# A graph-attention layer on one core: one wait per operation, rings of eight, destinations over 102 partitions

## Chip, core and metric

The kernel runs on 1 core of one Trainium2 chip. The metric is device time in microseconds (us), the median of 3 runs; lower is better.

## What is computed

The reference is one graph-attention layer with a residual and a layer norm. N = 12500 nodes have 96 features; E = 412500 edges are sorted by destination; there are 8 heads of 12 features.

```python
Q, K, V = x @ Wq + bq, x @ Wk + bk, x @ Wv + bv         # (N, 8, 12) each
Ee      = edge_attr @ We + be                            # (E, 8, 12)
score = exp(clip(sum(K[src] * Q[dst] / sqrt(12) * Ee, over 12), -5, 5))
wV = segment_sum(V[src] * score, dst, N)
Z  = segment_sum(score, dst, N)
out = layernorm(x + wV / (Z + 1e-6))
```

## The kernel before

**Tiling.** The edges go in C = 806 chunks of 512 edges, four groups of 128 (G = 4). As the edges are sorted, the destinations of one chunk nearly always lie in one window of 32 nodes (WIN), so a chunk's queries are picked, and its messages summed, by matmuls with one-hot matrices. Weights and sums are float32; the query table is kept as three bfloat16 parts, hence 96 rows (SEL = 32 x 3) of a one-hot for the queries.

**Stages.** A first stage (about 160 us) makes the K/V and Q tables in HBM, the tables of windows and indices, and a copy of the destinations as 16-bit numbers. The main stage runs 806 steps, one per chunk. The last stage divides by Z and normalizes.

**One step of the main stage**, each engine in its own order, tied by semaphores alone (no planner; the order is written out by hand in one `step` function per engine):

- POOL (L546) issues four indirect DMAs (L553) that gather the 512 rows of K and V (768 bytes each) into one of 8 slots (RING). For the gather of chunk s it waits until the messages of chunk s - 8 are made (`msg_ready` >= s - 7), so it runs at most seven chunks ahead of the messages. This wait is the same before and after.
- SP (L412) loads the query windows four at a time, when `pe_step` allows.
- ACT (L784) for step s: waits for `pe_step` >= s + 1 and for `score_ready`, makes the exponential of chunk s - 1 (L791), waits that one-hot t has been made, makes the transposed one-hot of chunk s + 4 in two activations (L798, L801), issues the load of four chunks of destinations (L376, every fourth step), copies indices (L757, every fourth), and issues the load of four chunks of edge attributes (L361, three DMAs, every fourth step, after a wait on `ea_turned`).
- PE (L655) for step s: the edge projection (L665, 4 matmuls that appear as 8, float32 in two passes), the query selection (L670, 4), and the summing of chunk s - 5 (L678, shown as 8). The last one raises `pe_step`. There is no wait inside the summing.
- DVE (L930) for step s: waits for `pe_step` >= s + 1 and for the gather of chunk s, then kqe = k x q (L944), the one-hot of chunk s - 1 (L947), kqe x e (L952), messages of chunk s - 1 (L956, after the exponential; raises `msg_ready`), the reduction over 12 (L963), the addition into the accumulator (L971), the clip (L975), and the transposition of the attributes of chunk s + 4 (L980, raises `ea_turned`).

Rings before: one-hots for queries 4 (`ohT`), messages 4 (`msg`), one-hots for sums 4, attributes 16, destinations 8, indices 16.

At the start SP issues two groups of attributes and two of destinations (L419 to L423) before it stores the query table (L428).

## Time and profile before

| | |
|---|---|
| median of 3 runs | 5284.68 us (5274.52 to 5292.71) |
| the profiled execution | 5282.84 us |
| its span, first to last instruction | 5281.0 us |
| mean granted TensorE clock | 0.507 of full speed |
| busy: PE / DVE / ACT / POOL | 59% / 47% / 25% / 60% |
| mean HBM traffic | 115 GB/s |

No engine is busy for more than 60% of the span, and the shares are flat over it. The page's part 4, the chain of waits that ended last, tells which engine the time follows; the view of waits tells what each engine waited for; the timelines show one round of the pipeline. "issue" is time in which an engine waited for nothing that the profile shows; "remote" is a release of which the profile does not show the sender.

### The profile page before, as it was taken

The page shows a single profiled execution, that of the slowest core. Times are in us where ns is not written, and L with a number is a line of the kernel's source. Part 1 is how long each engine was busy: PE and PEld are TensorE (multiplying, and loading weights), DVE is VectorE, ACT ScalarE, POOL GpSimd, SP SyncE. Part 2 cuts the span into 40 slices and gives each one's busy share as a digit, 9 for nine tenths or more (in the row PEclk, how much of TensorE's full clock was granted, in tenths as well). Part 3 has the DMA queues.
Part 4 walks back from the last instruction along what each step waited for, and adds up shares of the span by engine and source line. Part 5 has one row for each costly group of instructions (what it writes and reads, how often), then busy time and mean ns, then how long its engine had stood idle before and what let it go on. Part 6 is the DMA issues. An engine that isn't in the chain of part 4 may idle for free.

```text
span 5281.0 us, 65022 instructions
## 1 busy us (share of the span) xinstructions
PE 3108.9 (59%) x16776; PEld 3038.4 (58%) x16777; DVE 2471.5 (47%) x6851; ACT 1338.4 (25%) x2885; POOL 3184.4 (60%) x3332
## 2 busy tenths in 40 slices
PE   6656556556565556655565555655555556665655
PEld 5655555555565555555565555555555555565555
DVE  3544444444444444444444444444444444444446
ACT  3322222222222222222222222222222222222224
POOL 4465666666656666666666666666566656666664
PEclk7555555555555555555555555555555555555555
DMA  7654545554544554444555544455444545454443
GB/s 211 136 113 109 114 111 114 113 115 109 117 112 110 114 114 114 110 111 110 116 113 114 114 110 111 112 114 114 109 114 111 115 111 115 110 117 110 112 108 97
DMA packets 1532837, 607.55 MB, mean 115 GB/s; under 512 B 1394171, under 2 KB 1455174, under 8 KB 1532579
## 3 DMA queue, kind: packets, MB, share of 16 engines
q10 hardware_dynamic: 1245734, 233.93, 23.6%
q0 software_dynamic: 155616, 321.69, 23.0%
q1 hardware_dynamic: 131459, 51.62, 4.0%
q8 instruction: 9, 0.15, 0.0%
q14 instruction: 19, 0.16, 0.0%
HBM read 584.51 MB, written 22.46 MB: 115 GB/s over the span
## 4 chain that ended last, share of the span: by engine, by line
PE 55%; issue 40%; DVE 1%; another core or an unknown queue 1%; DMA 1%; SPq 1%; ACT 0%; DVEq 0%; POOL 0%; ACTq 0%; POOLq 0%
PE bank L665 28%; PE bank L678 21%; PE bank L670 5%; DMA kv_mem<-in_x_dram 1%; PE bank L613 0%; DVE y_stats L1060 0%; SPq L361 0%; DMA q_table<-ea_mem 0%; SPq L395 0%; DVE kqe L952 0%; DVE raw_score L963 0%; SPq L428 0%; SPq L381 0%; DVE z_inv L1049 0%
## 5 line engine op out<-in xcount | busy, mean ns | idle before, releaser
L553 POOL DMA_INDIRECT kv_mem<-kv_table,src_idx x3224 | 3117.8, 967 | 2037.2 <-DVE msg L956 1043.3
L678 PE MATMUL bank<-oh,msg 128*104 128x32 f32 x6448 | 1302.8, 337 | 1611.2 <-issue 1610.5
L678 PEld LDWEIGHTS bank<-oh,msg 128*104 128x104 f32 x6448 | 1282.1, 285 | 1586.5 <-issue 1585.4
L665 PE MATMUL bank<-w_e,eaT 97*128 97x96 f32 x6448 | 1663.8, 429 | 328.1 <-issue 321.8
L665 PEld LDWEIGHTS bank<-w_e,eaT 97*128 97x128 f32 x6448 | 1494.7, 330 | 400.6 <-issue 399.0
L944 DVE TENSOR_TENSOR kqe<-kv_mem,bank 128x384 f32<-128x384 f32 x806 | 427.8, 531 | 2677.1 <-remote 2133.4
L791 ACT ACTIVATE msg<-score 128x32 f32<-128x32 f32 x806 | 184.9, 229 | 3798.9 <-remote 2633.6
L798 ACT ACTIVATE away<-dst_b,minus_id 96x512 bf16<-96x512 int16 x806 | 572.4, 710 | 6.1 <-PE bank L670 3.6
L980 DVE STREAM_TRANSPOSE eaT<-ea_mem 96x512 f32<-96x512 f32 x806 | 564.3, 700 | 0.0
L670 PE MATMUL bank<-q_win,ohT 96*128 96x96 bf16 x3224 | 449.0, 280 | 144.2 <-issue 138.4
L801 ACT ACTIVATE ohT<-away 96x512 bf16<-96x512 bf16 x806 | 507.5, 630 | 25.4
L670 PEld LDWEIGHTS bank<-q_win,ohT 96*128 96x128 bf16 x3224 | 410.4, 157 | 154.7 <-issue 146.3
L956 DVE TENSOR_TENSOR msg<-kv_mem,msg 128x384 f32<-128x384 f32 x806 | 441.7, 548 | 16.9 <-issue 12.9
L963 DVE TENSOR_REDUCE raw_score<-kqe 128x32 f32<-128x384 f32 x806 | 438.1, 544 | 0.0
L952 DVE TENSOR_TENSOR kqe<-kqe,bank 128x384 f32<-128x384 f32 x806 | 437.6, 543 | 0.0
L947 DVE TENSOR_TENSOR oh<-iota,rel 128x128 f32<-128x128 f32 x806 | 223.9, 278 | 0.0
L975 DVE TENSOR_SCALAR score<-raw_score 128x32 f32<-128x32 f32 x806 | 183.0, 227 | 0.2
L971 DVE TENSOR_TENSOR accT<-bank,accT 104x32 f32 x806 | 144.3, 179 | 4.1 <-PE bank L678 2.9
L639 PE MATMUL bank<-w_kvq,accT 97*125 97x96 f32 x200 | 37.5, 373 | 30.2 <-issue 17.8
L639 PEld LDWEIGHTS bank<-w_kvq,accT 97*125 97x125 f32 x200 | 36.1, 285 | 31.7 <-issue 19.4
L576 POOL TENSOR_TENSOR kv_mem<-kv_mem,spare 125x384 f32<-125x384 f32 x25 | 25.0, 999 | 44.5 <-DVE kv_mem L1054 44.5
L724 PE MATMUL bank<-ident,accT 104*125 104x104 f32 x100 | 30.6, 464 | 25.2 <-DVE kv_mem L1054 23.0
(90 smaller groups left out, 473.1 us busy)
## 6 DMA issues: line engine op xcount, KB each, us to landing
ea_mem<-in_edge_attr_dram ACTq DMA_DIRECT2D x591, 256.0 KB
dst_b<-dst_by_chunk ACTq DMA_DIRECT2D x199, 384.0 KB
kv_mem<-kv_table,src_idx POOLq DMA_INDIRECT x3224
q_win<-q_table SPq DMA_DIRECT2D x806, 19.9 KB
kv_table<-kv_mem SPq DMA_DIRECT2D x25, 336.0 KB
q_table<-ea_mem SPq DMA_DIRECT2D x25, 252.0 KB
kv_mem<-in_x_dram SPq DMA_DIRECT2D x25, 168.0 KB
spare<-in_x_dram SPq DMA_DIRECT2D x25, 168.0 KB
```

The costliest lines, as they stand in the source:

```text
L553: pool.indirect_dma_start(kv[:, slot, g, :], None, kv_dram[:, :], bass.IndirectOffsetOnAxis(ap=src_idx[:, u, g:g + 1], axis=0)).then_inc(k ...
L665: nc.tensor.matmul(e_ps[v][:, g * D:(g + 1) * D], eaT[:, v, g * P:(g + 1) * P], w_e[:, :], start=True, stop=True)
L670: last = nc.tensor.matmul(q_ps[v][:, g * D:(g + 1) * D], ohT[:, v, g * P:(g + 1) * P], q_win[0:SEL, u, :], start=(g == 0), stop=(g == G - ...
L678: last = nc.tensor.matmul(sum_ps[v], msg[:, w, g, :], oh[:, w, g, :], start=(g == 0), stop=(g == G - 1), skip_group_check=True)
L798: nc.scalar.activation(away[:, :], dst_b[:, w, :], ACT.Abs, bias=minus_id[:, bass.ds(t, 1)]).then_inc(away_done, 1)
L801: nc.scalar.activation(ohT[:, v, :], away[:, :], ACT.Relu, bias=1.0, scale=-1.0).then_inc(ohT_built, 1)
L944: nc.vector.tensor_tensor(kqe[:, :, :], kv[:, ua, :, 0:D], q_ps[v][:, 0:G * D].rearrange("p (g d) -> p g d", g=G), ALU.mult).then_inc(kq_d ...
L947: nc.vector.tensor_tensor(oh[:, um % DEPTH, :, :], iota[:, 0:WIN].unsqueeze(1).to_broadcast((P, G, WIN)), rel[:, bass.ds(m * G, G)].unsque ...
L952: nc.vector.tensor_tensor(kqe[:, :, :], kqe[:, :, :], e_ps[v].rearrange("p (g d) -> p g d", g=G), ALU.mult).then_inc(kqe_done, 1)
L956: nc.vector.tensor_tensor(msg[:, um % DEPTH, :, 0:D].rearrange("p g (h d) -> p g h d", d=HD), kv[:, um, :, D:2 * D].rearrange("p g (h d) - ...
L963: nc.vector.tensor_reduce(raw_score[:, :], kqe[:, :, :].rearrange("p g (h d) -> p (g h) d", d=HD), AX_X, ALU.add).then_inc(heads_summed, 1)
L980: nc.vector.transpose(eaT[0:D, v, :], ea[:, w, :]).then_inc(ea_turned, 1)
```

## The change

What it does, part by part:

1. PE: the wait for the query one-hot (`ohT_built`) moves from the query matmuls to the second group of the edge projection; in the steps after the last chunk the wait on `acc_added` goes.
2. ACT: the waits on `pe_step` and on `ohT_built` go; `away` has two buffers; `ohT` has eight (MSG_RING); the attribute loads are issued one residue earlier (u % 4 == 0, 16 chunks ahead, not 15), and their wait on `ea_turned` goes except at step 0.
3. DVE: new order of the same eight operations: one-hot, accumulator addition, k x q, x e, messages, reduction, transposition, clip. The waits on its own `heads_summed`, `acc_added` and on `exp_done` before the clip go; one wait on `score_ready` stands before the addition. The one-hot raises no semaphore.
4. `msg` has eight buffers, not four.
5. The destinations are loaded into 102 partitions, not 96.
6. Start: SP waits for the stored destinations first, loads attribute group 0 alone, and group 1 only after the query table is stored, with groups 2 and 3. Several small buffers share memory.

```diff
@@ load_destinations
-                "(a c r) -> a c r", a=1, c=count).to_broadcast((SEL, count, CHUNK))).then_inc(dst_b_in[h], 16)
+                "(a c r) -> a c r", a=1, c=count).to_broadcast((SEL_LOAD, count, CHUNK))).then_inc(dst_b_in[h], 16)
@@ sync
             sp.wait_ge(src_turned, NJ)
+            sp.wait_ge(dst16_stored, 32)
             load_edges(sp, 0, 0)
-            sp.wait_ge(dst16_stored, 32)
-            load_edges(sp, EA_GROUP, 1)
...
-            for g in range(2, EA_RING // EA_GROUP):
+            for g in range(1, EA_RING // EA_GROUP):
                 load_edges(sp, g * EA_GROUP, g)
@@ tensor: step
                     for g in range(G):
+                        if g == 1:
+                            pe.wait_ge(ohT_built, s + 1)
                         nc.tensor.matmul(e_ps[v][:, g * D:(g + 1) * D], eaT[:, v, g * P:(g + 1) * P],
                                          w_e[:, :], start=True, stop=True)
-                    pe.wait_ge(ohT_built, s + 1)
                     landed(pe, q_win_in, s, u, 16)
...
-                    pe.wait_ge(acc_added, n - DEPTH + 1)
                     pe.wait_ge(msg_ready, n + 1)
@@ scalar: step
-                m, t, v = s - 1, s + DEPTH, u % DEPTH
-                if not isinstance(s, int) or s >= 0:
-                    act.wait_ge(pe_step, s + 1)
+                m, t, w = s - 1, s + DEPTH, (u + DEPTH) % RING
                 if not isinstance(s, int) or 0 <= m < C:
                     act.wait_ge(score_ready, m + 1)
...
-                    at_least(act, ohT_built, t)
-                    nc.scalar.activation(away[:, :], dst_b[:, w, :], ACT.Abs,
+                    nc.scalar.activation(away[:, u % 2, :], dst_b[0:SEL, w, :], ACT.Abs,
                                          bias=minus_id[:, bass.ds(t, 1)]).then_inc(away_done, 1)
                     act.wait_ge(away_done, t + 1)
-                    nc.scalar.activation(ohT[:, v, :], away[:, :], ACT.Relu, bias=1.0, scale=-1.0).then_inc(ohT_built, 1)
+                    nc.scalar.activation(ohT[:, w, :], away[:, u % 2, :], ACT.Relu, bias=1.0, scale=-1.0).then_inc(ohT_built, 1)
...
-                if u % EA_GROUP == 1 and (not isinstance(s, int) or 0 <= s and s + EA_AHEAD < C):
-                    act.wait_ge(ea_turned, s + EA_AHEAD - EA_RING + EA_GROUP)
+                if u % EA_GROUP == EA_AHEAD % EA_GROUP and (not isinstance(s, int) or 0 <= s and s + EA_AHEAD < C):
+                    if isinstance(s, int) and s == 0:
+                        act.wait_ge(ea_turned, EA_GROUP)
                     load_edges(act, s + EA_AHEAD, (u + EA_AHEAD) % EA_RING // EA_GROUP)
@@ vector: step
                     dve.wait_ge(pe_step, a + 1)
-                if scores:
-                    landed(dve, kv_in, a, ua, 16 * G)
-                    at_least(dve, heads_summed, a)
-                    nc.vector.tensor_tensor(kqe[:, :, :], kv[:, ua, :, 0:D],
-                                            q_ps[v][:, 0:G * D].rearrange("p (g d) -> p g d", g=G), ALU.mult).then_inc(kq_done, 1)
                 if messages:
                     nc.vector.tensor_tensor(oh[:, um % DEPTH, :, :], iota[:, 0:WIN].unsqueeze(1).to_broadcast((P, G, WIN)),
                                             rel[:, bass.ds(m * G, G)].unsqueeze(2).to_broadcast((P, G, WIN)),
-                                            ALU.is_equal).then_inc(oh_built, 1)
+                                            ALU.is_equal)
+                if not isinstance(s, int) or 1 <= a <= C:
+
+                    dve.wait_ge(score_ready, a)
+                elif a > C:
+                    dve.wait_ge(acc_added, n)
+                if sums:
+                    if base is None:
+                        base = dve.value_load(base_tab[0:1, bass.ds(n, 1)], min_val=0, max_val=N - 1)
+                    acc = accT[0:DZ, bass.ds(base, WIN)]
+                    nc.vector.tensor_tensor(acc, sum_ps[v], acc, ALU.add).then_inc(acc_added, 1)
                 if scores:
+                    landed(dve, kv_in, a, ua, 16 * G)
+                    nc.vector.tensor_tensor(kqe[:, :, :], kv[:, ua, :, 0:D],
+                                            q_ps[v][:, 0:G * D].rearrange("p (g d) -> p g d", g=G), ALU.mult).then_inc(kq_done, 1)
                     dve.wait_ge(kq_done, a + 1)
                     nc.vector.tensor_tensor(kqe[:, :, :], kqe[:, :, :],
                                             e_ps[v].rearrange("p (g d) -> p g d", g=G), ALU.mult).then_inc(kqe_done, 1)
                 if messages:
                     dve.wait_ge(exp_done, m + 1)
-                    nc.vector.tensor_tensor(msg[:, um % DEPTH, :, 0:D].rearrange("p g (h d) -> p g h d", d=HD),
+                    nc.vector.tensor_tensor(msg[:, um % MSG_RING, :, 0:D].rearrange("p g (h d) -> p g h d", d=HD),
                                             kv[:, um, :, D:2 * D].rearrange("p g (h d) -> p g h d", d=HD),
-                                            msg[:, um % DEPTH, :, D:DZ].unsqueeze(3).to_broadcast((P, G, HEADS, HD)),
+                                            msg[:, um % MSG_RING, :, D:DZ].unsqueeze(3).to_broadcast((P, G, HEADS, HD)),
                                             ALU.mult).then_inc(msg_ready, 1)
                 if scores:
                     dve.wait_ge(kqe_done, a + 1)
-                    at_least(dve, score_ready, a)
                     nc.vector.tensor_reduce(raw_score[:, :], kqe[:, :, :].rearrange("p g (h d) -> p (g h) d", d=HD),
                                             AX_X, ALU.add).then_inc(heads_summed, 1)
-                if sums:
-
-                    if base is None:
-                        base = dve.value_load(base_tab[0:1, bass.ds(n, 1)], min_val=0, max_val=N - 1)
-                    at_least(dve, acc_added, n)
-                    acc = accT[0:DZ, bass.ds(base, WIN)]
-                    nc.vector.tensor_tensor(acc, sum_ps[v], acc, ALU.add).then_inc(acc_added, 1)
-                if scores:
-                    dve.wait_ge(heads_summed, a + 1)
-                    at_least(dve, exp_done, a - 1)
-                    nc.vector.tensor_scalar(score[:, ua % 2, :], raw_score[:, :], -5.0, 5.0, ALU.max, ALU.min).then_inc(score_ready, 1)
                 if not isinstance(s, int) or t < C:
                     w = (u + DEPTH) % EA_RING
                     if w % EA_GROUP == 0:
                         landed_edges(dve, t, w)
                     nc.vector.transpose(eaT[0:D, v, :], ea[:, w, :]).then_inc(ea_turned, 1)
+                if scores:
+                    dve.wait_ge(heads_summed, a + 1)
+                    nc.vector.tensor_scalar(score[:, ua % 2, :], raw_score[:, :], -5.0, 5.0, ALU.max, ALU.min).then_inc(score_ready, 1)
```

## Rows read from the trace of the kernel before

**Rows 1.** The page: busy times, and the chain that ended last.
```profile
PE 3108.9 (59%) x16776; PEld 3038.4 (58%) x16777; DVE 2471.5 (47%) x6851; ACT 1338.4 (25%) x2885; POOL 3184.4 (60%) x3332
...
PE 55%; issue 40%; DVE 1%; another core or an unknown queue 1%; DMA 1%; SPq 1%; ACT 0%; DVEq 0%; POOL 0%; ACTq 0%; POOLq 0%
```
**Rows 2.** Windows: stretch, length, busy us (x instructions) per engine, clock, DMA share, GB/s.
```profile
50.00:100.00 50.00, 37.59 (x272) 34.77 (x272) 17.27 (x28) 24.93 (x53) 8.70 (x10) 0.94 0.85 224
...
2000.00:3000.00 1000.00, 587.78 (x3179) 577.19 (x3178) 464.84 (x1274) 241.88 (x517) 613.73 (x636) 0.50 0.50 113
```
**Rows 3.** Waits, 2000 to 3000 us: engine, line, releaser: us in total, times, longest.
```profile
ACT msg L791 <- remote: 511.7, 50, 15.5
DVE kqe L944 <- remote: 414.7, 48, 13.7
...
POOL kv_mem L553 <- DVE msg L956: 197.2, 47, 5.8
```
**Rows 4.** Timeline of POOL, one round: start, us, operation, [idle before <- releaser].
```profile
2591.29 0.95 POOL L553 DMA_INDIRECT kv_mem<-kv_table,src_idx  x1 [5.13 <-DVE msg L956]
...
2610.32 0.95 POOL L553 DMA_INDIRECT kv_mem<-kv_table,src_idx  x1 [0.30 <-issue]
2616.48 0.95 POOL L553 DMA_INDIRECT kv_mem<-kv_table,src_idx  x1 [5.20 <-DVE msg L956]
```
**Rows 5.** Timeline of PE, same round.
```profile
2592.51 2.00 PE L665 MATMUL bank<-w_e,eaT 97*128 97x96 f32 x8
...
2596.01 2.00 PE L665 MATMUL bank<-w_e,eaT 97*128 97x96 f32 x8
...
2604.76 0.21 PE L678 MATMUL bank<-oh,msg 128*104 128x32 f32 x1 [1.76 <-issue]
...
2613.88 1.81 PE L665 MATMUL bank<-w_e,eaT 97*128 97x96 f32 x8 [1.18 <-issue]
```
**Rows 6.** Timeline of DVE, same round.
```profile
2601.22 0.56 DVE L944 TENSOR_TENSOR kqe<-kv_mem,bank 128x384 f32<-128x384 f32 x1 [3.73 <-remote]
...
2613.98 0.56 DVE L944 TENSOR_TENSOR kqe<-kv_mem,bank 128x384 f32<-128x384 f32 x1 [9.78 <-PE bank L678]
2614.45 0.28 DVE L947 TENSOR_TENSOR oh<-iota,rel 128x128 f32<-128x128 f32 x1
2614.65 0.55 DVE L952 TENSOR_TENSOR kqe<-kqe,bank 128x384 f32<-128x384 f32 x1
2615.12 0.55 DVE L956 TENSOR_TENSOR msg<-kv_mem,msg 128x384 f32<-128x384 f32 x1
2615.59 0.55 DVE L963 TENSOR_REDUCE raw_score<-kqe 128x32 f32<-128x384 f32 x1
2616.05 0.18 DVE L971 TENSOR_TENSOR accT<-bank,accT 104x32 f32 x1
2616.16 0.18 DVE L975 TENSOR_SCALAR score<-raw_score 128x32 f32<-128x32 f32 x1
```
**Rows 7.** Timeline of ACT and its queue, same round: loads of attributes and destinations.
```profile
2602.25 3.38 ACTq L361 DMA_DIRECT2D ea_mem<-in_edge_attr_dram  x3
...
2617.45 0.33 ACTq L376 DMA_DIRECT2D dst_b<-dst_by_chunk  x1
```
**Rows 8.** Timelines of the last rounds: last attribute load, POOL, PE.
```profile
5121.79 3.02 ACTq L361 DMA_DIRECT2D ea_mem<-in_edge_attr_dram  x6
...
5164.10 0.95 POOL L553 DMA_INDIRECT kv_mem<-kv_table,src_idx  x1 [5.22 <-DVE msg L956]
...
5177.58 0.21 PE L678 MATMUL bank<-oh,msg 128*104 128x32 f32 x1 [1.75 <-issue]
...
5189.31 0.95 POOL L553 DMA_INDIRECT kv_mem<-kv_table,src_idx  x1 [5.25 <-DVE msg L956]
```
**Rows 9.** Timelines of SP's queue and DVE in the first stage.
```profile
83.75 10.13 SPq L361 DMA_DIRECT2D ea_mem<-in_edge_attr_dram  x6
...
96.30 59.97 SPq L428 DMA_DIRECT2D q_table<-ea_mem  x50
...
103.01 0.56 DVE L916 TENSOR_TENSOR q_rest<-bank,ea_mem 125x384 f32<-125x384 f32 x1 [13.24 <-issue]
```

More of the change, by code:

```diff
@@ L22 @@
 DEPTH = 4
+MSG_RING = 8
 OUT_RING = 8
@@ L27 @@
 SEL_READ = 106
+SEL_LOAD = 102
 RING = 8
@@ L31 @@
 EA_GROUP = 4
-EA_AHEAD = EA_RING - 1
+EA_AHEAD = 16
 IDX_RING = 16
@@ L131, in gnn_kernel @@
             "p (u j k d) -> p u j k d", j=BATCH, k=PARTS, d=D)
-        q_rest = sb("q_rest", [P, 2, BATCH, D])
+        msg_mem = sb("msg_mem", [P, MSG_RING * G * DZ])
+        msg = msg_mem[:, :].rearrange("p (c g f) -> p c g f", g=G, f=DZ)
+        q_rest = msg_mem[:, 0:2 * BATCH * D].rearrange("p (u j d) -> p u j d", j=BATCH, d=D)
         zero = sb("zero", [P, 1])
@@ L139, in gnn_kernel @@
         dst_nat = spare[0:NQ, 0:NJ * CHUNK]
-        dst16_end = sb("dst16_end", [1, CHUNK], I16)
-        dst_end_row = sb("dst_end_row", [1, CHUNK], I32)
+        dst_end_row = kv_mem[0:1, 12 * BATCH * D:12 * BATCH * D + CHUNK].bitcast(I32)
+        dst16_end = kv_mem[0:1, 12 * BATCH * D + CHUNK:12 * BATCH * D + CHUNK * 3 // 2].bitcast(I16)
         dst_end = sb("dst_end", [P, G], I32)
@@ L154, in gnn_kernel @@
         src_tab = sb("src_tab", [P, C * G])
-        dst_b = sb("dst_b", [SEL, RING, CHUNK], I16)
+        dst_b = sb("dst_b", [SEL_LOAD, RING, CHUNK], I16)
         q_win = sb("q_win", [SEL_READ, RING, D], BF16)
@@ L159, in gnn_kernel @@
         eaT = sb("eaT", [DA, DEPTH, CHUNK])
-        away = sb("away", [SEL, CHUNK], BF16)
-        ohT = sb("ohT", [SEL, DEPTH, CHUNK], BF16)
+        away = sb("away", [SEL, 2, CHUNK], BF16)
+        ohT = sb("ohT", [SEL, MSG_RING, CHUNK], BF16)
         oh = sb("oh", [P, DEPTH, G, WIN])
@@ L165, in gnn_kernel @@
         score = sb("score", [P, 2, G * HEADS])
-        msg = sb("msg", [P, DEPTH, G, DZ])
         f_node_id = sb("f_node_id", [SEL, 1])
-        f_ohT = sb("f_ohT", [SEL, CHUNK], BF16)
+        f_ohT = away[:, 0, :]
         f_rel = sb("f_rel", [P, G])
-        f_oh = sb("f_oh", [P, G, WIN])
+        f_oh = oh[:, 0, :, :]
         x_res = spare[:, 0:4 * BATCH * D].rearrange("p (u j d) -> p u j d", j=BATCH, d=D)
@@ L248, in gnn_kernel @@
         exp_done = sem("exp_done")
-        oh_built = sem("oh_built")
         msg_ready = sem("msg_ready")
@@ L664, in step @@
                     for g in range(G):
+                        if g == 1:
+                            pe.wait_ge(ohT_built, s + 1)
                         nc.tensor.matmul(e_ps[v][:, g * D:(g + 1) * D], eaT[:, v, g * P:(g + 1) * P],
                                          w_e[:, :], start=True, stop=True)
-                    pe.wait_ge(ohT_built, s + 1)
                     landed(pe, q_win_in, s, u, 16)
                     for g in range(G):
-                        last = nc.tensor.matmul(q_ps[v][:, g * D:(g + 1) * D], ohT[:, v, g * P:(g + 1) * P], q_win[0:SEL, u, :],
+                        last = nc.tensor.matmul(q_ps[v][:, g * D:(g + 1) * D], ohT[:, u, g * P:(g + 1) * P], q_win[0:SEL, u, :],
                                                 start=(g == 0), stop=(g == G - 1), skip_group_check=True)
                 else:
-                    pe.wait_ge(acc_added, n - DEPTH + 1)
                     pe.wait_ge(msg_ready, n + 1)
@@ L677, in step @@
                     for g in range(G):
-                        last = nc.tensor.matmul(sum_ps[v], msg[:, w, g, :], oh[:, w, g, :],
+                        last = nc.tensor.matmul(sum_ps[v], msg[:, w, g, :], oh[:, w % DEPTH, g, :],
                                                 start=(g == 0), stop=(g == G - 1), skip_group_check=True)
@@ L689, in add_queries @@
                     for g in range(G):
-                        last = nc.tensor.matmul(q_ps[0][:, g * D:(g + 1) * D], f_ohT[:, g * P:(g + 1) * P], q_win[0:SEL, 0, :],
+                        last = nc.tensor.matmul(q_ps[0][:, g * D:(g + 1) * D], away[:, 0, g * P:(g + 1) * P], q_win[0:SEL, 0, :],
                                                 start=first and g == 0, stop=(g == G - 1), skip_group_check=True)
@@ L705, in further @@
                     for g in range(G):
-                        last = nc.tensor.matmul(sum_ps[1], msg[:, 0, g, :], f_oh[:, g, :],
+                        last = nc.tensor.matmul(sum_ps[1], msg[:, 0, g, :], oh[:, 0, g, :],
                                                 start=(g == 0), stop=(g == G - 1))
@@ L980, in step @@
                     nc.vector.transpose(eaT[0:D, v, :], ea[:, w, :]).then_inc(ea_turned, 1)
+                if scores:
+                    dve.wait_ge(heads_summed, a + 1)
+                    nc.vector.tensor_scalar(score[:, ua % 2, :], raw_score[:, :], -5.0, 5.0, ALU.max, ALU.min).then_inc(score_ready, 1)
             run_steps(dve, step, C, SUM_LAG, lambda i: [base for k in range(2) for base in load_bases(dve, i * EA_RING + k * RING - SUM_LAG)],
-                      lead=DEPTH, unroll=EA_RING, ahead=DEPTH)
+                      lead=DEPTH, unroll=EA_RING, ahead=DEPTH + EA_GROUP)
             def further(c, extra):
```

21 lines of the change are left out of this document (10 added, 11 removed).

## The prediction

> **What bounds the kernel now.** I read the page first. PE and POOL are busy 59% and 60%, DVE 47%, ACT 25%, and the chain that ended last is PE's: 55% work and 40% "issue", time in which PE waits for nothing the profile shows [rows 1]. So no engine is full, and no semaphore of the program explains the gaps. By windows the main stage is uniform: every stretch has the shares and the clock of the one from 2000 to 3000 us [rows 2], so one round, read closely, stands for all.
>
> The waits of that stretch name the partners: ACT and DVE together wait for a "remote" release (511.7 and 414.7 us of 1000), and POOL 197.2 us for the messages of DVE, in 47 waits of which the longest is 5.8 us [rows 3]. The timelines put these in order. A round is four chunks. POOL starts at 2591.29, issues 16 gathers one after another (the last at 2610.32, so 1.27 us each, 5.07 us a chunk), stands for 5.20 us, and starts again at 2616.48 [rows 4]: 25.19 us a round, 6.30 us a chunk, times 806 = 5076 us; the other 207 us of the profiled execution (5282.84 us) are the first and last stage. That execution stands 1.8 us below the median of the runs.
>
> Why does POOL stand? It is seven chunks ahead and needs the next messages. DVE has begun its step at 2601.22 and again only at 2613.98, after 9.78 us idle [rows 6]; that wait is the one on `pe_step`. PE does a step in 3.50 us when it runs (2592.51 to 2596.01), but from about 2602 on its matmuls start 1.2 to 2.6 us apart, in the middle of the summing, where there is no wait at all (1.76 us idle ahead of the one at 2604.76), and all is released at once at 2613.88 [rows 5]: 2.6 us after POOL's last gather ended (2611.28). PE and its signals are held while gathers run, and let go when they pause. What the hardware does there the trace does not say. That it is the gathers and no other transfer the last rounds show: the attributes' last load is issued at 5121.79 to 5124.81, and still the rounds after it are 25.21 us (5164.10 to 5189.31) with the same idle (5.22, 5.25 us) and the same gaps in PE (1.75 us) [rows 8].
>
> So the time is: rounds x (16 gathers + the pause), and the pause is landing (2.6 us after the last gather), then DVE from its release to the messages, then POOL's start.
>
> **The change part by part.**
>
> *DVE's order.* After the release at 2613.98 the messages start at 2615.12, 1.14 us later, and the gather 1.36 us after that [rows 4, 6]. Before the messages stand k x q, one-hot, x e: 0.47 + 0.20 + 0.47 us from start to start. After the change they are one-hot, accumulator addition, k x q, x e: 0.20 + 0.11 + k x q + 0.47. The addition, 0.11 us (2616.05 to 2616.16), used to come behind the messages and now stands ahead. And x e now follows k x q directly, which it must wait for; the one-hot stood between them. From below, k x q costs its old pitch, 0.47: messages 1.25 us after the release, +0.11. From above, a dependent operation starts when the one before it has ended: reduction at 2615.59, 0.55 long, clip at 2616.16, 0.57 from start to start although the addition stands between [rows 6]; k x q, 0.56 long, then costs 0.58, and the messages come at 1.36: +0.22. If the new wait on `score_ready` ahead of the addition is also seen, some 0.02 more. I take +0.23 us, by the row of the dependent clip. There are 806/4 = 201 rounds: +46 us; from below 22, and from above, if two such handovers of 0.1 are paid, 66.
>
> A DVE step in full becomes about 3.05 us (from 2.90), still under PE's 3.50: no cost off the release. In the step itself the transposition now comes before the clip, the messages' exponential gets its input 0.6 us later; DVE needs it after 1.3 us of the next step, and ACT takes 0.2: covered by that.
>
> *Waits and semaphores dropped.* On ACT (25% busy) the wait on `pe_step` goes, so the exponential of the held step is done early; but DVE waits for `pe_step` itself ahead of the messages, so nothing is released sooner: 0. Cover gone, that is if ACT were late, it would cost at most its 1.3 us of two activations; it has 5 to 11 us of idle a round. On PE one semaphore instruction per step goes: while PE runs, 40 weight loads and matmuls fill the 3.50 us without a gap [rows 5], so 0; while it is held, an item fewer could let it get 0.7 to 1.4 us further, which the round does not see, as POOL's pause ends it. Queued behind PE's new early wait for the one-hot are three groups of the projection; ACT makes that one-hot four chunks ahead: 0. The wait on `score_ready` at DVE's addition is on its own last operation, priced above.
>
> *Rings of eight.* Neither the messages nor the one-hots of four were waited for by name; PE sums five chunks behind. 0. POOL's allowance is the ring of gathered rows, which stays 8.
>
> *Attributes one residue earlier.* The three DMAs were issued at 2602.25, inside the hold; they will now go out about 6 us earlier, beside running gathers, right behind the step that loads destinations [rows 7]. POOL's pitch is the same with them and without (1.27 us), and the hold is the same without them [rows 8]: 0 for the round. What they may do is delay PE's third signal of a round, a rival below.
>
> *Destinations over 102 partitions.* One load per four chunks, issued in 0.33 us [rows 7], needed five steps (some 30 us) later; hidden by that. 
>
> *Start.* SP issued six attribute DMAs for 10.13 us before the query table, whose stores begin at 96.30, while DVE stands 13.24 us [rows 9]. Three of the six move behind the stores: about -5 us, and +5 us where DVE then needs group 1 (as much from the other side: -5 to +5). I take 0.
>
> Sum: 5282.84 + 46 = 5329, and with the median's 1.8 us 5331 us, +0.9%. Its own range, by the bounds 22 and 66 and the start's 5 either way, is 5302 to 5356.
>
> **Rivals.** A run within 0.3% (16 us) of the median before cannot be told from no change.
>
> *No change* (0.20): DVE's longer path is made up, by a hold that ends earlier or by PE's missing instruction. For it: these are tenths of a microsecond. Against it: POOL's pause follows DVE's release at a fixed distance. 5285 us.
>
> *Five chunks a round* (0.29, faster): a pause costs 4.90 us whatever it ends. In a round three of PE's signals arrive while gathers run and the fourth is held. PE with an instruction less, and with no attributes loading in its hold, may get so far ahead that the fourth arrives. Then a round is 5 x 5.07 + 5.13 = 30.5 us, 6.10 us a chunk: 4917 + 207 = 5124 us if all are so, between that and 5270 if some are. For it: in the last rounds, with no attributes to load, PE does more within the hold. Against: they still had four chunks.
>
> *The holds vanish* (0.06, faster): POOL's 5.07 us a chunk bound, 4086 + 207 = 4293 us. The granted clock was 0.94 from 50 to 100 us, with PE busy 75%, and 0.50 at 59% [rows 2], so PE would speed up too. The Trainium skill, "TensorE: Matmul & The Clock Gate", "Why this matters for your kernels", would have it so, since it ties full clock to work without gaps; by it nothing changes while the holds stay. Against: the gathers are untouched.
>
> *Three chunks a round* (0.08, slower): the attribute load now runs at the time of PE's third signal, which already came late (DVE idle 3.73 us at 2601.22 [rows 6]). If it misses the point where POOL has issued three chunks after its restart less the 2.5 us from signal to gather, some 12.7 us, every round ends a chunk early: 3 x 5.07 + 5.13 = 20.3 us, 6.78 a chunk, 5465 + 207 = 5672 us.
>
> *The forecast* has 0.37.
>
> **How the numbers follow.** Faster by over 0.3%: 0.29 + 0.06 = 0.35. Within: 0.20. Slower: 0.37 + 0.08 = 0.45. The likeliest case gives 5331 us. The range takes in that case, no change and five chunks in any share of the rounds, down to 5120, and on top some rounds of three, up to 5410; outside lie the vanished holds and most of the rounds of three.
>
> **What would show it.** Right: DVE's timeline after a wait of 10 us reads one-hot, addition, k x q, x e, messages, with the messages 1.3 to 1.4 us after the release; POOL's pause is 5.4 us after every 16 gathers; PE's issue share stays near 40%; the clock stays 0.50. Wrong: pauses after 20 or 12 gathers, a pause that isn't longer, POOL without pauses, or PE without the gaps in the summing.

## The result and the profile after

The changed kernel takes 5304.34 us (median of 6 runs, 5298.10 to 5311.64) against 5284.73 us (6 runs, 5274.52 to 5294.05) on the same chip: ratio 1.0033, 95% interval 1.0020 to 1.0046. It is slower, by 20 us; the forecast was 46. The profiled execution spans 5302.6 us, 22 more than before.

The page: busy times, the chain that ended last, and the group of the gathers (busy us, mean ns of one | idle before, releaser). To set beside [rows 1].
```profile
PE 3184.9 (60%) x16776; PEld 3052.3 (58%) x16777; DVE 2540.2 (48%) x6851; ACT 1327.6 (25%) x2885; POOL 3215.7 (61%) x3332
...
PE 47%; issue 35%; DVE 7%; another core or an unknown queue 7%; DVEq 1%; DMA 1%; SPq 1%; ACT 0%; ACTq 0%; POOL 0%; POOLq 0%
...
L555 POOL DMA_INDIRECT kv_mem<-kv_table,src_idx x3224 | 3149.1, 977 | 2024.4 <-DVE msg_mem L962 991.5
```
The shares are close to those of before; the chain has less of PE (47% for 55%) and of issue (35% for 40%), and more of DVE and of releases whose sender the profile doesn't show. One row I had not asked about: POOL's busy time is 31 us longer with the same 3224 gathers. One takes 977 ns, before 967 (3117.8 us in all).

Windows, 2000 to 3000 us (as [rows 2]), and the waits of that stretch (as [rows 3]).
```profile
2000.00:3000.00 1000.00, 604.76 (x3176) 579.64 (x3175) 480.64 (x1276) 239.54 (x517) 618.09 (x634) 0.50 0.54 114
```
```profile
DVE oh L940 <- remote: 388.8, 42, 13.7
...
POOL kv_mem L555 <- DVE msg_mem L962: 190.4, 42, 6.2
```
634 gathers in 1000 us, before 636; POOL stands for the messages 42 times instead of 47, the longest time 6.2 us instead of 5.8. Fewer and longer waits.

DVE's timeline behind a hold, the answer to [rows 6].
```profile
2621.67 0.29 DVE L940 TENSOR_TENSOR oh<-iota,rel 128x128 f32<-128x128 f32 x1 [13.16 <-remote]
2621.88 0.18 DVE L952 TENSOR_TENSOR accT<-bank,accT 104x32 f32 x1
2621.98 0.55 DVE L955 TENSOR_TENSOR kqe<-kv_mem,bank 128x384 f32<-128x384 f32 x1
2622.56 0.55 DVE L958 TENSOR_TENSOR kqe<-kqe,bank 128x384 f32<-128x384 f32 x1
2623.03 0.55 DVE L962 TENSOR_TENSOR msg_mem<-kv_mem,msg_mem 128x384 f32<-128x384 f32 x1
```
The release, at which the one-hot starts, to the messages is 1.36 us (before 1.14), and k x q to x e 0.58: the numbers forecast. But POOL's timeline around it no longer has a pause after every 16 gathers (as [rows 4]; rows behind a pause):
```profile
2563.33 1.02 POOL L555 DMA_INDIRECT kv_mem<-kv_table,src_idx  x1 [5.23 <-DVE msg_mem L962]
2588.84 0.95 POOL L555 DMA_INDIRECT kv_mem<-kv_table,src_idx  x1 [5.63 <-DVE msg_mem L962]
2595.96 1.01 POOL L555 DMA_INDIRECT kv_mem<-kv_table,src_idx  x1 [2.40 <-DVE msg_mem L962]
2624.48 0.95 POOL L555 DMA_INDIRECT kv_mem<-kv_table,src_idx  x1 [2.92 <-issue]
2644.67 1.01 POOL L555 DMA_INDIRECT kv_mem<-kv_table,src_idx  x1 [4.33 <-DVE msg_mem L962]
```
Taken over the main stage (gathers that start between 250 and 5000 us; a round ends where POOL stands over 1 us; its pause is that stand without the 0.30 us that lie between any two gathers; medians of the rounds of four):
```
                rounds of 4      median round   gathers   pause    rounds of 5   round
before          162              25.25 us       20.36     4.90      4            31.0
after            96              25.58          20.38     5.19     45            31.3
a chunk, all rounds: before 6.300 us, after 6.308 us
```
A round of four is 0.33 us longer. But 31.3 us for five is 6.26 a chunk, below the 6.31 of before. The rest are odd rounds, 19 of a single chunk among them (before 10), and 17 of the rounds of four are under 24.5 us (before 5).

The books of the whole stage, from the first gather behind the filled ring to the last, show what this adds up to: POOL stands over 3 us 169 times instead of 193, for 5.42 us each instead of 5.13. These long stands make 74 us less; short ones of 1 to 3 us make 48 us more, and the longer gathers 31. So the stage is 5.6 us longer in all.

The rest lies in the first stage. SP's queue, DVE and POOL, to set beside [rows 9]:
```profile
85.32 4.12 SPq L363 DMA_DIRECT2D ea_mem<-in_edge_attr_dram  x3
...
90.95 68.02 SPq L430 DMA_DIRECT2D q_table<-ea_mem  x50
162.21 8.92 SPq L410 DMA_DIRECT2D q_win<-q_table  x8
...
167.34 0.55 DVE L955 TENSOR_TENSOR kqe<-kv_mem,bank 128x384 f32<-128x384 f32 x1 [7.48 <-PE bank L673]
...
178.35 0.71 DVE L974 STREAM_TRANSPOSE eaT<-ea_mem 96x512 f32<-96x512 f32 x1 [9.28 <-DMA ea_mem<-in_edge_attr_dram]
181.67 0.95 POOL L555 DMA_INDIRECT kv_mem<-kv_table,src_idx  x1 [50.10 <-DVE msg_mem L962]
```
The 50 stores of the query table take 68.0 us instead of 60.0, although they begin 5.4 us earlier, and the transposition of chunk 4 waits 9.28 us for attributes that used to be there. The first gather behind the filled ring starts at 181.67, before at 167.94: +13.7 us. In the kernel before, the first k x q reads:
```profile
162.98 0.56 DVE L944 TENSOR_TENSOR kqe<-kv_mem,bank 128x384 f32<-128x384 f32 x1 [5.83 <-PE bank L670]
```
So 4.4 of the 13.7 us pass ahead of the first k x q (167.34 for 162.98), and 9.4 between it and that gather (14.33 us for 4.97), where the transposition waits. Together: 13.7 (start) + 5.6 (rounds) + 2.2 (behind the last gather) = 21.5 of 21.6 us.

### The profile page after: what moved, and what is told of

Its sections match the earlier page's. It is cut to its first block, busy times and chain, and to the rows that moved or that the text cites. A ratio compares the mean times of both kernels' runs of the same rounds, so it can differ in the third digit from the quotient of the medians.

```text
span 5302.6 us, 60807 instructions
## 1 busy us (share of the span) xinstructions
PE 3184.9 (60%) x16776; PEld 3052.3 (58%) x16777; DVE 2540.2 (48%) x6851; ACT 1327.6 (25%) x2885; POOL 3215.7 (61%) x3332
## 4 chain that ended last, share of the span: by engine, by line
PE 47%; issue 35%; DVE 7%; another core or an unknown queue 7%; DVEq 1%; DMA 1%; SPq 1%; ACT 0%; ACTq 0%; POOL 0%; POOLq 0%
PE bank L669 24%; PE bank L679 18%; PE bank L673 5%; DVE kqe L958 1%; DVE raw_score L968 1%; DVE kqe L955 1%; DVE msg_mem L962 1%; DVEq L318 1%; DMA kv_mem<-in_x_dram 1%; DVE accT L952 0%; DVE eaT L974 0%; DVE score L977 0%; PE bank L615 0%; DVE y_stats L1057 0%
## 5 line engine op out<-in xcount | busy, mean ns | idle before, releaser
L669 PE MATMUL bank<-w_e,eaT 97*128 97x96 f32 x6448 | 1699.9, 425 | 609.7 <-issue 586.8
L679 PE MATMUL bank<-oh,msg_mem 128*104 128x32 f32 x6448 | 1310.8, 342 | 1125.2 <-issue 1121.9
L679 PEld LDWEIGHTS bank<-oh,msg_mem 128*104 128x104 f32 x6448 | 1270.5, 286 | 1120.7 <-issue 1117.0
L669 PEld LDWEIGHTS bank<-w_e,eaT 97*128 97x128 f32 x6448 | 1513.9, 327 | 686.9 <-issue 668.5
L790 ACT ACTIVATE msg_mem<-score 128x32 f32<-128x32 f32 x806 | 184.8, 229 | 3835.8 <-DVE score L977 2495.1
L673 PE MATMUL bank<-q_win,ohT 96*128 96x96 bf16 x3224 | 460.6, 278 | 293.1 <-issue 285.9
L962 DVE TENSOR_TENSOR msg_mem<-kv_mem,msg_mem 128x384 f32<-128x384 f32 x806 | 447.8, 556 | 55.9 <-issue 42.3
L955 DVE TENSOR_TENSOR kqe<-kv_mem,bank 128x384 f32<-128x384 f32 x806 | 438.9, 545 | 7.7 <-PE bank L673 7.5
L977 DVE TENSOR_SCALAR score<-raw_score 128x32 f32<-128x32 f32 x806 | 147.6, 183 | 0.1
```

Of the source, the lines that this page charges most:

```text
L669: nc.tensor.matmul(e_ps[v][:, g * D:(g + 1) * D], eaT[:, v, g * P:(g + 1) * P], w_e[:, :], start=True, stop=True)
L673: last = nc.tensor.matmul(q_ps[v][:, g * D:(g + 1) * D], ohT[:, u, g * P:(g + 1) * P], q_win[0:SEL, u, :], start=(g == 0), stop=(g == G - ...
L679: last = nc.tensor.matmul(sum_ps[v], msg[:, w, g, :], oh[:, w % DEPTH, g, :], start=(g == 0), stop=(g == G - 1), skip_group_check=True)
L955: nc.vector.tensor_tensor(kqe[:, :, :], kv[:, ua, :, 0:D], q_ps[v][:, 0:G * D].rearrange("p (g d) -> p g d", g=G), ALU.mult).then_inc(kq_d ...
L962: nc.vector.tensor_tensor(msg[:, um % MSG_RING, :, 0:D].rearrange("p g (h d) -> p g h d", d=HD), kv[:, um, :, D:2 * D].rearrange("p g (h d ...
```

## The experiments

The kernels ran in five groups, each group on one chip: the kernel before took 5350, 4289, 5283, 4288 and 5343 us in them. The record numbers the chip 0, 0, 0, 12 and 6, which doesn't say whether the first three were the same one; so it stays open whether the groups differ by the chip or by a state of it. Where the text says a chip with or without pauses, it means such a group. So each kernel is compared with the kernel before of its own group. In the second and fourth POOL never pauses; what that means stands further down.

**a_oldstart**: the changed kernel with SP's old order.
```diff
-            sp.wait_ge(dst16_stored, 32)
             load_edges(sp, 0, 0)
+            sp.wait_ge(dst16_stored, 32)
+            load_edges(sp, EA_GROUP, 1)
```

> The changed kernel with one thing undone: SP issues the attributes of groups 0 and 1 ahead of the query table's stores, as the kernel before did; groups 2 and 3 behind. Theory T (the 20 us of the change are 14 us of start, and a steady part in which DVE's longer way to the messages and rounds of five chunks nearly cancel): the first gather behind the ring's fill moves from 181.7 us back to about 168, the rounds stay as they are (99 of 4, 46 of 5), and the time falls by 14 us, to about 5290 us, 1.001 of the kernel before. Rival S (the early start is only waited off elsewhere, in the first round): no change, 5304 us.

Measured 0.9983 (0.9971 to 0.9994). The transposition no longer waits for attributes:
```profile
172.70 0.55 DVE L956 TENSOR_TENSOR kqe<-kv_mem,bank 128x384 f32<-128x384 f32 x1 [7.85 <-PE bank L674]
```
From this first k x q to the first gather behind the ring (177.66) are 4.96 us, as in the kernel before. But the first k x q itself is late, so that gather is not at 168 as expected; b_newdve, on the same chip with 96 partitions, has it at 171.59. The rounds didn't stay as they were either: 107 of four, 24 of five, 17 of three. The time fell more than the start explains (a rough 0.5% below the changed kernel's ratio of another group); the surplus stays open.

**b_newdve**: the kernel before with DVE's new order alone (the DVE part of the change's diff).

> The kernel before with DVE's new order alone (one-hot, addition, k x q, x e, messages, reduction, transposition, clip; rings, ACT, PE, attributes and start as before). Theory T: POOL's pauses grow by 0.22 us to 5.4, rounds stay at 4 chunks as before (at most 20 rounds of 5), time +0.22 x 201 = +44 us, about 5329 us (1.008). Rival R1 (the order itself makes rounds of five, because DVE hands PE its transposed attributes earlier in the step): a third of the rounds have five chunks and the time is about 5290 us (1.001). Rival R2 (the release path doesn't set the pause): 5285 us with rounds of 4.

Measured 1.0025 (1.0016 to 1.0034), +12 us. The traced execution, the fastest of eleven and 14 us under their median, has 18 rounds of five. That lies between theory T (up to 20 of them, 1.008) and R1 (a third of the rounds, 1.001).

**c_olddve**: everything changed but DVE's order.
```diff
-  (one-hot, addition, k x q, x e, messages, reduction, transposition, clip)
+  (k x q, one-hot, x e, messages, reduction, addition, clip, transposition)
-                    if isinstance(s, int) and s == 0:
-                        act.wait_ge(ea_turned, EA_GROUP)
+                    act.wait_ge(ea_turned, s + EA_GROUP)
```

> The changed kernel with DVE's old order and its waits (k x q, one-hot, x e, messages, reduction, addition, clip, transposition); rings of eight, ACT, PE, attribute timing, destinations and start stay changed. ACT gets a wait on the transposed attributes before each attribute load, since the order of clip and transposition no longer stands in for it. Theory T: if the rounds of five come from ACT, PE or the attribute loads, they stay (46 of 5 or more) and pauses shrink to 5.2 us: 5304 - 44 = about 5260 us (0.995). Rival R1 (the fives come from DVE's order): rounds of 4 only, pauses 5.2: 5285 + 14 of start = about 5299 us (1.003).

Measured 1.0034 (1.0021 to 1.0047): 181 rounds of four, none of five, as R1 has it. In this group the two kernels with DVE's new order have fives, a_oldstart 24 and b_newdve, which adds nothing but the order, 18. PE with an instruction less, one half of my reason for fives, is refuted: that is in this kernel. The other half, no attributes in the hold, is not: with the restored wait the attribute loads go out 12 to 14 us behind POOL's restart in 145 of the 181 rounds of four, and PE's hold lasts from some 10 to 22 us behind it; in the changed kernel their median is 7.7 us. Most of what it loses is the start: its first gather behind the ring is at 185.8, 14.2 us behind that of b_newdve. Beside b_newdve on the same chip it also gives the forecast's term by itself: median round of four 25.53 against 25.75 us, +0.22.

**d_msgfirst**: old start, messages at the head of DVE's step.
```diff
                 dve.wait_ge(pe_step, a + 1)
                 one-hot
+                dve.wait_ge(exp_done, m + 1)
+                messages
                 k x q; addition; x e
-                messages
                 reduction; transposition; clip
```
(In PE's tail, waits on `acc_added` and `kqe_done` come with it.)

> The changed kernel with the old start and DVE's messages moved to the head of the step, behind the wait on PE's step and the one-hot alone (then k x q, addition, x e, reduction, transposition, clip); all the work stays. The exponential of the held step is done early, as ACT no longer waits for PE's step. Theory T (the pause is the release plus DVE's way to the messages): messages start 0.2 us after the release instead of 1.36, pauses fall from 5.6 to about 4.4 us, time 5290 - 1.16 x 195 = about 5064 us (0.958) if the rounds keep their chunks; if the shorter pause gives PE less time and all rounds fall back to 4 chunks, 4 x 5.07 + 4.4 = 24.7 us a round, 6.17 a chunk, 5180 us (0.98); with some rounds of 3, up to 5290. Rival R2 (the release path doesn't set the pause): 5290 us.

Measured 0.9731 (0.9718 to 0.9743). Pauses of rounds of four are 4.46 us, against 5.32 in b_newdve on the same chip. The distance from release to messages sets the pause; that part of the forecast's mechanism is shown by shortening it. 79 rounds of three are the predicted price of the shorter pause.

**e_turnearly, f_turnlast, g_msgturn, after_again**, one group:
```diff
 e (kernel before):      reduction; addition;
-                        clip; transposition
+                        transposition; clip
 f (new order of DVE):
-                        transposition; clip
+                        clip; transposition
 g (d_msgfirst):
-                        reduction; transposition; clip
+                        transposition; reduction; clip
```

> The kernel before with one thing moved: DVE's transposition stands ahead of the clip instead of behind it; all else is as before. Theory T (rounds of five come from the transposition's place: PE gets the attributes of its next step 0.2 us earlier and one more signal slips through before the hold; and it alone): some 20 rounds of 5 appear as in the run with DVE's new order, pauses stay what they are in the kernel before, and the time falls below it, by about 30 us (0.994). Rival R1 (the fives come from the later messages, that is from the longer pause, which gives PE more time): no fives, 1.000. Rival R2 (a later clip makes the exponential late and the pause longer): 1.002 to 1.005.

> The kernel before with DVE's new order (one-hot, addition, k x q, x e, messages, reduction, clip) except that the transposition stays last. Theory T (fives from the transposition's place): no fives, all rounds 4, pauses 0.2 us longer than the kernel before has: +44 us, 1.008. Rival R1 (fives from the longer pause): 20 or more rounds of 5 as with the whole new order, 1.0025.

> The messages-first kernel (old start, messages right behind PE's step and the one-hot) with the transposition moved ahead of the reduction, 0.55 us earlier in the step. Theory T (an earlier transposition lets PE get further in the window before the hold): fewer rounds of 3 (79 there), more of 5, pauses still 4.4 us: about 5160 us, 0.965 of the kernel before. Rival (the rounds are set by how long the window is, not by the transposition): 0.973 as there. Rival 2 (the clip now follows the reduction it depends on, and the exponential arrives late for the messages): 0.975 to 0.985.

> The changed kernel itself, so that it stands beside the others of this call. Both theories: 1.0033 of the kernel before within 0.0013; more rounds of 5 than the kernel before, in which pauses of 5.3 to 5.5 us prevail.

The kernel before took 4289 us here, and not one of the four traces has a pause: the stage is gathers end to end. That is the rival "the holds vanish", for which I had worked out 4293 us; but the unchanged kernel shows it too, so it isn't the change that does it. Measured: e 1.0021 (1.0012 to 1.0030), f 1.0182 (1.0168 to 1.0196), g 0.9954 (0.9941 to 0.9968), after_again 1.0249 (1.0233 to 1.0265). Nobody had forecast that. The gather's group on the four pages, in this order:
```profile
L553 POOL DMA_INDIRECT kv_mem<-kv_table,src_idx x3224 | 3123.9, 969 | 1054.2 <-issue 951.4
```
```profile
L553 POOL DMA_INDIRECT kv_mem<-kv_table,src_idx x3224 | 3192.2, 990 | 1054.5 <-issue 971.0
```
```profile
L556 POOL DMA_INDIRECT kv_mem<-kv_table,src_idx x3224 | 3090.8, 959 | 1065.7 <-issue 930.8
```
```profile
L555 POOL DMA_INDIRECT kv_mem<-kv_table,src_idx x3224 | 3214.9, 997 | 1065.0 <-issue 948.0
```
The times follow the mean length of a gather: 28 ns x 3224 = 91 us between e and after_again, and the start's 11.5 us (166.0 against 154.5) make 102, where their medians are 101.5 apart. What stretches a gather shows in the changed kernel's first trace too. POOL, then DVE:
```profile
2602.46 1.03 POOL L555 DMA_INDIRECT kv_mem<-kv_table,src_idx  x1 [0.30 <-issue]
2603.80 1.34 POOL L555 DMA_INDIRECT kv_mem<-kv_table,src_idx  x1 [0.31 <-issue]
2605.44 1.03 POOL L555 DMA_INDIRECT kv_mem<-kv_table,src_idx  x1 [0.30 <-issue]
2606.78 0.95 POOL L555 DMA_INDIRECT kv_mem<-kv_table,src_idx  x1 [0.30 <-issue]
```
```profile
2604.69 0.70 DVE L974 STREAM_TRANSPOSE eaT<-ea_mem 96x512 f32<-96x512 f32 x1
2605.32 0.14 DVE L977 TENSOR_SCALAR score<-raw_score 128x32 f32<-128x32 f32 x1
```
A transposition begins 0.89 us into a gather, and the gather takes 1.34 us instead of 0.95. Sorted by that offset, over after_again from 250 to 4000 us (mean start to start of the gather in which the transposition begins):
```
offset, us     0.0-0.4   0.5     0.6     0.7     0.8     0.9 and later
gathers, n     186       33      26      46      237     194
pitch, us      1.257     1.309   1.397   1.502   1.612   1.258
```
If the transposition begins before a point some 0.9 us into the gather, the gather ends 0.45 us after that beginning, or at its usual time if that is later; if it begins behind the point, the gather is not touched. In e_turnearly the point lies 1.0 us in (the gather ends 0.35 us after the beginning) and 220 transpositions begin between 1.0 and 1.1 us, just behind it; in after_again 237 begin just ahead of theirs. DVE mostly waits there for gathers that land, so it keeps its phase to POOL, and the same operation falls on the same spot of the gather for hundreds of chunks. The Trainium skill, "SBUF — State Buffer", section "SBUF: two separate sides", says that while DVE runs an operation in a mode that takes two ports, GpSimd can't write the descriptors of its DMAs. It doesn't name the transposition, and the trace agrees only in part: the transposition does stretch gathers (+0.39 us at most), but a stretched gather ends 0.25 us before the transposition does (2605.14 against 2605.39 above). So that this is the cause is not shown. The addition stretches a gather by up to 0.08 us; k x q, x e, messages and reduction leave gathers at 1.258 us.

**i_split, j_msgsplit, k_dst96, before_again**, one group; POOL pauses here.
```diff
 i (changed kernel), j (g_msgturn):
-                    nc.vector.transpose(eaT[0:D, v, :], ea[:, w, :]).then_inc(ea_turned, 1)
+                    nc.vector.transpose(eaT[0:D, v, 0:CHUNK // 2], ea[:, w, 0:CHUNK // 2])
+                    nc.vector.transpose(eaT[0:D, v, CHUNK // 2:CHUNK], ea[:, w, CHUNK // 2:CHUNK]).then_inc(ea_turned, 1)
 k (changed kernel):
-SEL_LOAD = 102
+SEL_LOAD = 96
```

> The changed kernel with DVE's transposition of a chunk (0.70 us) done in two halves of 256 columns, one behind the other; nothing else. Theory T (a gather has a point, 0.9 to 1.1 us after its start, at which it waits for a transposition that DVE has begun, and stretches from 1.258 to up to 1.64 us; the changed kernel's order puts the transposition on that point in a quarter of the gathers): the gather gets in between the halves, so none stretches beyond about 1.35, and the mean pitch of gathers falls from 1.30 or 1.28 to about 1.27 us; the time falls below the changed kernel's by 0.5% or more (where gathers run without pauses by 1.5%: from 1.025 to about 1.010 of the kernel before). Rival (the stretch has another cause, or the two halves hold as one): pitch and time of the changed kernel stay (1.003 with pauses, 1.025 without), DVE's step 0.06 us longer.

Measured 1.0035 (1.0013 to 1.0056). The mean gather did fall to 967 ns, but not as expected: with the first half beginning 0.8 us in, the pitch is 1.610, as with the whole. Two halves hold as one; what had changed is how many transpositions meet the spot (213 instead of 268 begin 0.5 to 0.9 us into a gather). And the time didn't follow the gathers: where POOL pauses, a longer gather and a shorter pause make up for each other in part.

> Messages first, transposition ahead of the reduction and in two halves, old start; a version that is to beat both kernels. Theory T: where POOL pauses, 0.970 or less of the kernel before; where it doesn't, pitch 1.258 to 1.262 us and 0.995. Rival (the halves cost DVE more than they give): 0.975 and 0.998.

Measured 0.9726 (0.9712 to 0.9739), 5139 us: faster than both kernels. POOL and DVE:
```profile
2608.73 0.95 POOL L556 DMA_INDIRECT kv_mem<-kv_table,src_idx  x1 [4.50 <-DVE msg_mem L948]
2633.18 0.95 POOL L556 DMA_INDIRECT kv_mem<-kv_table,src_idx  x1 [4.39 <-DVE msg_mem L948]
```
```profile
2607.16 0.29 DVE L943 TENSOR_TENSOR oh<-iota,rel 128x128 f32<-128x128 f32 x1 [9.71 <-remote]
2607.37 0.55 DVE L948 TENSOR_TENSOR msg_mem<-kv_mem,msg_mem 128x384 f32<-128x384 f32 x1
```
Messages come 0.21 us behind the release and POOL 1.36 us behind them. 185 rounds of four at 24.43 us, against 25.23 in before_again: 0.80 x 201 = 161 us less, 144 measured.

> The changed kernel with destinations loaded over 96 partitions instead of 102; nothing else. Theory T (the load is early by 30 us, however many engines carry it): the same as the changed kernel within 0.15% (1.0033 of the kernel before with pauses, 1.025 without). Rival D (102 partitions spread the load otherwise and free or fill queues that gathers and attributes use): off the changed kernel by over 0.3% either way.

Measured 1.0008 (0.9999 to 1.0017). Against i_split of the same group, SP's queue in k, then in i:
```profile
91.53 63.18 SPq L430 DMA_DIRECT2D q_table<-ea_mem  x50
157.93 7.15 SPq L410 DMA_DIRECT2D q_win<-q_table  x8
```
```profile
91.96 69.78 SPq L430 DMA_DIRECT2D q_table<-ea_mem  x50
164.95 8.92 SPq L410 DMA_DIRECT2D q_win<-q_table  x8
```
The two destination loads stand right ahead of these stores; over 102 partitions the stores take 6.6 us and the query loads 1.8 us longer, and the first gather behind the ring comes at 184.65 instead of 175.68. So the load's width costs the start up to 9 us here (i also has the halves; 6 us by a against b, where 2.4 of them are a later begin of the stores). The rest of the difference in time, 5 of 14 us by the two ratios, is within the intervals. Against the changed kernel's 1.0033 it is 0.25% less, more than the 0.15% that theory T allowed and less than rival D's 0.3%: the load was early for its own reader, and still cost time. before_again gave 1.0007 and repeated the kernel before: 170 rounds of four, 3 of five, the first gather behind the ring at 169.34.

**e2_turnearly, f2_turnlast, after_third, l_quarter**: the next group met a chip without pauses again, and repeated 1.0023, 1.0183 and 1.0259 (each within 0.0010 of the first). l_quarter leaves out three of the four gathers of a chunk behind the first eight chunks:
```diff
-                for g in range(G):
+                for g in range(G if isinstance(s, int) and s < RING else 1):
```

> The changed kernel with one gather of four per chunk behind the first eight chunks (the other three quarters of each chunk's rows are left out, so keys and values there are stale): POOL needs 1.27 us a chunk, all else works on as before. Theory T (PE and its signals are held while gathers run, and POOL must pause often now): holds nearly vanish and PE's or DVE's own step bounds: 3.5 us a chunk, 806 x 3.5 + 220 = about 3050 us. Rival H (PE's gaps have nothing to do with gathers, another traffic or PE itself makes them): PE still needs about 6 us a chunk, over 4500 us.

Measured 3051.8 us; the page's busy times:
```profile
PE 2949.4 (97%) x16776; PEld 2927.7 (96%) x16777; DVE 2515.3 (82%) x6851; ACT 1328.1 (44%) x2885; POOL 882.1 (29%) x938
```
PE bounds at 3.49 us a chunk, as the step of [rows 5]. It says nothing of the holds, for there were none in that group to take away. It does say something of the clock: PE is busy for all of the 1000 us from 1000 to 2000, and the granted clock there is 0.50, the lower of its two levels (1.2 GHz).

**e3_turnearly, i2_split**: the same two kernels once more, on a chip with pauses.

> The kernel before with the transposition ahead of the clip, all else as before. On a chip with pauses, theory T (its place makes the fives): 20 or more rounds of 5 and 0.994 to 0.998 of the kernel before; rival R1 (the longer pause makes them): 5 or fewer rounds of 5, 0.998 to 1.003. On a chip without pauses: 1.002 again.

Measured 0.9977 (0.9968 to 0.9986), with 2 rounds of five and 42 of three. It doesn't settle whether the transposition's place makes fives: i2_split, with DVE's whole new order, has only 2 in this group as well. Why the time fell is open too.

> The changed kernel with the transposition in two halves. On a chip without pauses, theory T (a gather whose sensitive point falls into a transposition waits for its end): gathers stretch to 1.35 us at most where the two halves let one in between, mean pitch 1.30 falls to 1.27 to 1.28, time from 1.025 to about 1.010 of the kernel before; if the two halves hold as one, 1.025 stays, and 1.64 us remains the longest. Rival (another cause than the transposition): 1.025 with the stretched gathers where they were. On a chip with pauses: 1.0035 again.

Measured 1.0076 (1.0063 to 1.0089). 179 rounds are of four, 2 of five; the same kernel had 24 of five in the other group. This is the changed kernel, but for the halves, nearly without fives, and it comes near the forecast: +43 us, some 12 of them start (its first gather behind the ring is at 182.61, that of e3_turnearly at 170.61).

## Why the prediction was right and wrong

**The bound: right for this chip.** PE and its signals are held in the later part of a run of gathers, and POOL's pause is landing, release, DVE to the messages, restart. (In rounds of four PE starts 5 to 6 matmuls a us for some 9 us behind POOL's restart and mostly under 1 from 11 to 21 us, before and after alike, so gathers alone don't hold it from their start.) Lengthening DVE's way by 0.22 us lengthened the median round of four by 0.22 (c to b) and 0.33 (before to after); shortening it by 1.15 us shortened pauses by 0.9. In two of the groups there was no hold, at the same clock (0.51), though the gathers were the same. So the sentence "That it is the gathers" was too much: they are at most one of two conditions. The other is open; no run here told it. Nor did PE speed up where the holds were gone, as the rival "The holds vanish" expected: l_quarter's clock stayed at 0.50 with PE busy throughout. The page that the rival cites for it (the Trainium skill, "TensorE: Matmul & The Clock Gate", "Why this matters for your kernels") would have it otherwise; the measurement decides.

**DVE's order: right, 1.36 us, k x q at 0.58.**

**"There are 806/4 = 201 rounds: +46 us": the step that failed.** The price of a round held (0.22 to 0.33 us, forecast 0.23), their number didn't. At +0.33 us 201 rounds would have cost 66 us; some 45 rounds took five chunks, POOL stood long 24 times less, and the main stage became 5.6 us longer. I had the rival "five chunks a round", and put it at 0.29 as a case of its own, with some or all of the rounds at the old pause and a time of 5124 to 5270 us; what came was the forecast and the rival together, in one kernel. Its reason was at least in part wrong as well: not PE's missing instruction (c has that and not one five); the fives came with DVE's own new order (in c's group a has 24 and b 18). The order alone isn't enough, for i2_split has it and 2 fives. Whether the longer pause, the transposition's place or the moment of the attribute loads lets the extra signal through is open: the kernel that would tell of the first two (f) never met a chip with pauses, and c moved the loads as well.

**Start: sized 0, was +13.7 us.** The prediction had -5 us for stores that begin earlier and +5 where DVE then needs the second attribute group. The stores did begin 5.4 us earlier. But the wait for that group was 9.4 us, and it is SP's order that makes it: from the first k x q to the first gather behind the ring are 4.96 us in a_oldstart, 13.93 in c_olddve, which has the new start and DVE's old order, and 4.96 in b_newdve, so DVE's order costs nothing here. And the stores take 8.1 us longer and what lies from them to the first k x q 1.7, so that it comes 4.4 us later all the same. Inside one group the net of the two is +6.3 us without the wider load (k_dst96 against before_again) and up to +9.0 for its width (i_split against k_dst96).
**Not in the sum: the gather's length.** It grew by 10 ns, +31 us of POOL's busy time, which shorter standing paid back here; where POOL doesn't pause it was 28 ns and 91 us against e_turnearly. I had priced the transposition's move only on DVE.

**Waits dropped on ACT and rings in the main stage: 0**, as forecast: c has them, and beside the start's 14 of its 19 us only 5 are left. Attribute timing isn't separated, since c moved it again.

**The total.** That it came out slower at all rests on the start, 13.7 of 21.6 us, which the forecast had at nothing, while the term that it did price came to 5.6. The sign was right in part by luck.

## What to carry to other kernels

Where an engine's wait ends by another's release, count what stands between the release and the instruction that the bottleneck waits for, and put that instruction first: it gave 2.7% (d and j), where the change, which put one more operation and a direct dependence ahead of it, lost. A cycle whose length is whole chunks may jump to another count when its phase moves; price it as a mixture. A transfer that is early for its own reader can still delay whatever is queued behind it.

## What the hardware showed that I had not expected

The same kernel took 4288 to 4289 us in two groups and 5283 to 5350 us in three, each time steady within a few tenths of a per cent, with the clock at 0.51 in all. The change costs 0.33% in the one kind of group and 2.5% (1.0233 to 1.0273) in the other. And DVE's 0.70 us transposition stretches an indirect gather by up to 0.39 us, if it begins in the 0.4 us ahead of a point 0.9 to 1.0 us into the gather; cut in halves, it does the same.
